# Position distances from one minus the gate, rounded by ScalarE; turned outputs in a bank of their own; position logits of two units at once in the ring

## The chip, the cores and the metric
One core of a Trainium2 chip runs the whole decoder layer as one program. The metric is the device time of one execution in microseconds (us); the number given for a kernel is the median of its runs.

## The reference
x is 1x2048x256. The part that the change touches is the self-attention with 16 heads of 64, whose logits get a contextual position term (the cross-attention to 1601 context rows, the low-rank GELU network and the three layer norms are not touched):

```python
G = sigmoid(sim)                                   # sim = q k^T / 8, per head 2048 x 2048
P = flip(cumsum(flip(G)))                          # sum of the gates from j to the end of the row
P = minimum(P, 63)
E = einsum('bnc,ct->bnt', q, pos_emb)              # 64 position logits for each query
w = P - floor(P)
sim = sim + w * E[ceil(P)] + (1 - w) * E[floor(P)]
out = softmax(sim) @ v
```

Behind some 176 keys from the end the sum of gates is over 63 in all rows, so that the term is the constant E[63] there. The kernel subtracts E[63] from the table and works on the last W = 176 keys only. It keeps the lowest sum in satmin, and `general_attention` does the whole attention again if some row is not saturated at the window's start; with these inputs it doesn't.

## The kernel before, in words
A **unit** is 128 queries of one head, a **pair** is two units u = 0, 1. There are G = 16 x 8 = 128 pairs, and each engine runs its own program over them (`body(g)`; on SP, ScalarE (`act`), TensorE (`pe`) and VectorE (`dve`)). All order is written out by hand with semaphores; `wait_apart` is a wait as an instruction of its own. PSUM holds four banks of logits (`Sc`, one unit at a time), one of position logits (`near`), two of a ring (`ring`) and one of outputs (`out`). Ring slots are numbered: what TensorE puts there counts up `slot_full`, ScalarE's copy out of it counts up `slot_out`, and slot k waits until slot k - 2 is out.

In the pass for pair g, TensorE (L592 on) does: the logits of unit 0 in two halves (L544, each when ScalarE has read those banks for the unit before); the turn of pair g-1's unit 0 (L575: the outputs lie there as 64x2 halves by keys of even and odd tiles, and a matmul with `fold` adds and turns them); the 16 transposes of unit 1 of pair g-1 in four slots s0 to s3 (L552); its outputs (L566), interrupted by the queries and keys of the next head (`project`, L500) and the values (`project_values`, L513); the logits of unit 1; the turn of unit 1 of pair g-1; the transposes of unit 0 of pair g; the **window** (L522, position logits of pair g+2: 128 queries x 240 columns, 176 keys and 64 table entries, twice, both from the partitions 64 to 127 and into one bank); the outputs of unit 0.

ScalarE copies the ring out (`transposed` L409, `project` L368, `values` L382), scales the turned outputs by the inverse sum (`scale`, L418), copies `out` to `halves` (L424), does tanh on the window (L388), copies the table to z (L392), and the exponentials (L430, two halves of a row, each with its sum).

VectorE takes the maxima (L748), adds the correction to the last 175 logits (L755), finds the bias (L765), and works out the corrections of the next pair over 128x352 (two units of 176 keys): it scans tanh to 2P - 1 (L674), rounds (L680), runs a second scan that holds the floors to steps of one (L689), takes distances from a ramp (L695), makes seven bit masks (L702), shifts the table by each bit (`copy_predicated`, L712), takes clamp, fractions and slopes (L717, L722, L728), and shifts slopes and values by the last bit (L735, once per unit). GpSimd multiplies fractions and slopes (L348); VectorE adds (L742). SP loads the queries: `load_far` for the window two pairs ahead, `load_now` for the logits.

The loop has three stages: pairs 0 to 111 with project and values, 112 to 119 without values, 120 to 127 without both (`late`).

Of the kernel before, what the change touches and what calls it, by code (L numbers as in the profile page):

```python
# [44 lines left out]
RND2 = 1.5 * 2.0 ** 24  # L45
# [3 lines left out]
SATURATED = 2.0 * T - 3.0  # L49
SLOTS0 = 8 + 2 * PAIRS - 6  # L50
SLOTS = 12
LATE_SLOTS = 10
# [66 lines left out]
def attention(nc, A):  # L119
# [3 lines left out]
    with ExitStack() as ctx:  # L123
# [22 lines left out]
        q_far = sb("q_far", [P, 2 * P])  # L146
# [5 lines left out]
        twoP = sb("twoP", [P, 2, W])  # L152
        cut = sb("cut", [P, 2, W])
        rnd = sb("rnd", [P, 2, W])
        flo = rnd
        frac = cut
        dist = sb("dist", [P, 2, W], I16)
        mask = sb("mask", [P, BITS, 2, W], I16)
# [3 lines left out]
        ones = sb("ones", [P, W])  # L162
        twos = sb("twos", [P, W])
        ramp = sb("ramp", [P, 2, W])

        posx = cut[:, 0, 0:T]
        rampi = prod[:, :, :].bitcast(I32)
# [4 lines left out]
        near = pb("near", [P, BANK])  # L172
        ring = [pb(f"ring{i}", [P, BANK]) for i in range(2)]
        out = pb("out", [P, BANK])
        xs = probs[:, :, :].rearrange("p a (t d) -> p (a t) d", d=D)


        near_win = near[:, 0:2 * (W + T)].rearrange("p (i w) -> p i w", w=W + T)[:, :, 0:W]
        near_E = near[:, 0:2 * (W + T)].rearrange("p (i w) -> p i w", w=W + T)[:, :, W:W + T]
# [20 lines left out]
        halves_out = sem("halves_out")  # L200
        summed = sem("summed")
# [4 lines left out]
        shifted = sem("shifted")  # L206
        prod_done = sem("prod_done")
# [5 lines left out]
        def queries(h, odd, block):  # L213

            half = slice(0, C) if odd else slice(C, P)
            return qk[half, h % 2, int(odd), bass.ds(block // 2 * STEP, STEP)]

        SCANS = ["scan 0", "scan 1", "round"]
        SC = len(SCANS)
        CHAIN = (["floor 0", "floor 1", "distances", "cut"]  # L220
                 + [f"mask {b}" for b in reversed(range(BITS))]
                 + [f"shift {b}" for b in reversed(range(1, BITS))]
                 + ["fractions", "slopes", "last shift"])
# [3 lines left out]
        def _(sp):  # L227
# [51 lines left out]
            def body(g, odd, late=False, first=False, tile=True, far=True, head=False):  # L279
                base = slots_before(g, late)  # L280
                if head:

                    wait_apart(sp, out_full, g * 2, waited)
                    load_values(g)
# [1453 lines left out]
```

## Time and profile before
| | us |
|---|---|
| median of 3 runs | 2650.29 (2649.49 to 2651.93) |
| the profiled execution, its own time | 2652.94 |
| its span, first to last instruction | 2651.1 |
| TensorE busy | 2472.1 (93%) |
| VectorE busy | 2006.4 (76%) |
| ScalarE busy | 1615.9 (61%) |
| GpSimd busy | 190.4 (7%) |

The busy times are of the whole span; attention takes the first 2177 us of it, where all of the change lies. TensorE's granted clock has a mean of 0.985 of full speed. PE is TensorE's matmuls, PEld its weight loads, DVE VectorE, ACT ScalarE, POOL GpSimd.

### The profile page before, as it was taken

The page shows a single profiled execution, that of the slowest core. Times are in us where ns is not written, and L with a number is a line of the kernel's source. Part 1 is how long each engine was busy: PE and PEld are TensorE (multiplying, and loading weights), DVE is VectorE, ACT ScalarE, POOL GpSimd, SP SyncE. Part 2 cuts the span into 40 slices and gives each one's busy share as a digit, 9 for nine tenths or more (in the row PEclk, how much of TensorE's full clock was granted, in tenths as well). Part 3 has the DMA queues.
Part 4 walks back from the last instruction along what each step waited for, and adds up shares of the span by engine and source line. Part 5 has one row for each costly group of instructions (what it writes and reads, how often), then busy time and mean ns, then how long its engine had stood idle before and what let it go on. Part 6 is the DMA issues. An engine that isn't in the chain of part 4 may idle for free. (4 is left out here: it accounts for less than half of the span.)

```text
span 2651.1 us, 64197 instructions
## 1 busy us (share of the span) xinstructions
PE 2472.1 (93%) x18687; PEld 1691.1 (64%) x18687; DVE 2006.4 (76%) x5179; ACT 1615.9 (61%) x3383; POOL 190.4 (7%) x289
## 2 busy tenths in 40 slices
PE   7999998999899989998999999999999988999997
PEld 5666665666566656666666566666666656777776
DVE  6888888888888888888888888888899960232322
ACT  4666666666666666666666666666666663444442
POOL 0000000000000000000000000000000000111111
PEclk9999999999999999999999999999999998999998
DMA  2010101010101010100101110101001002100100
GB/s 68 20 33 20 34 20 32 20 34 20 32 20 34 20 32 21 32 21 21 29 24 29 25 29 24 29 24 29 22 21 40 21 17 68 34 26 34 36 26 6
DMA packets 96567, 74.74 MB, mean 28 GB/s; under 512 B 24590, under 2 KB 92303, under 8 KB 96464
## 3 DMA queue, kind: packets, MB, share of 16 engines
q1 hardware_dynamic: 96464, 73.15, 10.1%
q8 instruction: 90, 1.47, 0.2%
q14 instruction: 13, 0.11, 0.0%
HBM read 14.26 MB, written 2.10 MB: 6 GB/s over the span
## 5 line engine op out<-in xcount | busy, mean ns | idle before, releaser
L748 DVE TENSOR_REDUCE mx<-Sc 128x1 f32<-128x1024 f32 x512 | 621.5, 1214 | 160.2 <-PE Sc L544 159.7
L552 PE MATMUL ring<-ident,probs 128*128 128x128 f32 x4096 | 620.9, 284 | 115.2 <-ACT attn L418 65.3
L409 ACT ACTIVATE probsT<-ring 128x512 f32<-128x512 f32 x1024 | 584.7, 596 | 132.1 <-PE ring L552 129.2
L552 PEld LDWEIGHTS ring<-ident,probs 128*128 128x128 f32 x4096 | 446.3, 145 | 258.3 <-ACT attn L418 127.0
L430 ACT ACTIVATE probs<-Sc,nbias 128x1024 f32<-128x1024 f32 x512 | 565.6, 1117 | 4.7 <-DVE nbias L765 4.7
L544 PE MATMUL Sc<-qk,q_now 64*128 64x512 f32 x2048 | 539.4, 637 | 22.4 <-issue 16.0
L566 PE MATMUL out<-probsT,V_now 128*64 128x128 f32 x8192 | 530.0, 277 | 0.0
L566 PEld LDWEIGHTS out<-probsT,V_now 128*64 128x64 f32 x8192 | 439.5, 137 | 76.3 <-ACT probsT L409 57.9
L712 DVE COPY_PREDICATED z<-mask,z 128x224 f32<-128x224 int16 (+5 forms) x768 | 389.7, 507 | 34.4
L418 ACT ACTIVATE attn<-ring,rsum 128x64 f32 (+1 forms) x256 | 80.3, 314 | 436.5 <-PE ring L575 420.7
L544 PEld LDWEIGHTS Sc<-qk,q_now 64*128 64x128 f32 x2048 | 173.6, 188 | 217.8 <-issue 217.8
L348 POOL TENSOR_TENSOR prod<-cut,z 128x350 f32<-128x350 f32 x128 | 118.3, 924 | 2036.2 <-DVE z L735 2036.2
L575 PEld LDWEIGHTS ring<-fold,halves 128*128 128x128 f32 x512 | 76.9, 189 | 197.0 <-issue 114.6
L702 DVE TENSOR_SCALAR mask<-dist 128x352 int16<-128x352 int16 x896 | 155.3, 245 | 6.6
L500 PE MATMUL ring<-xT,wqk 128*128 (+1 forms) x512 | 144.3, 404 | 2.1 <-DMA wv<-in_L_attn_Wkv_dram 1.3
L522 PE MATMUL near<-qk,q_far 64*128 64x240 f32 x512 | 137.5, 389 | 2.0 <-DMA q_far<-qk 2.0
L674 DVE TENSOR_TENSOR_SCAN twoP<-tanh,ones 128x176 f32<-128x176 f32 x256 | 119.6, 510 | 12.6 <-ACT tanh L388 12.6
L735 DVE COPY_PREDICATED z<-mask,z 128x348 f32<-128x348 int16 x256 | 125.4, 544 | 0.1
L689 DVE TENSOR_TENSOR_SCAN rnd<-twos,rnd 128x176 f32<-128x176 f32 x256 | 118.9, 506 | 0.1
L424 ACT ACTIVATE halves<-out 128x128 f32<-128x128 f32 x256 | 72.1, 282 | 70.3 <-PE out L566 70.3
L575 PE MATMUL ring<-fold,halves 128*128 128x64 f32 x512 | 112.3, 301 | 1.6 <-ACT probs L430 1.2
L430 ACT ACTIVATION_READ_ACCUMULATOR probs<-Sc,nbias 128x1 f32 x512 | 108.1, 211 | 0.0
(116 smaller groups left out, 2301.8 us busy)
## 6 DMA issues: line engine op xcount, KB each, us to landing
q_now<-qk SPq DMA_DIRECT2D x256, 64.0 KB, 2.0
xv<-xT SPq DMA_DIRECT2D x113, 128.0 KB, 2.2
q_far<-qk SPq DMA_DIRECT2D x128, 64.0 KB, 1.9
V_now<-V SPq DMA_DIRECT2D x16, 512.0 KB, 3.2
at<-attn SPq DMA_DIRECT2D x16, 512.0 KB, 3.2
probs<-in_x_dram SPq DMA_DIRECT2D x4, 512.0 KB, 5.3
wqk<-in_L_attn_Wq_dram SPq DMA_DIRECT2D x32, 64.0 KB, 2.1
xin<-in_x_dram SPq DMA_DIRECT2D x16, 128.0 KB, 2.8
```

Of the source, the lines that this page charges most:

```text
L409: nc.scalar.activation(probsT[:, u, 4 * s:4 * s + 4, :], ring[k % 2][:, :].rearrange("p (t q) -> p t q", q=P), ACT.Copy).then_inc(slot_out, 1)
L430: nc.scalar.activation(probs[:, u, cols], Sc[:, cols], ACT.Exp, bias=nbias[:, u:u + 1], accum_out=sums[:, u, half:half + 1]).then_inc(exp_ ...
L500: last = nc.tensor.matmul(ring[k % 2][:, 0:STEP], wqk[:, c, at:at + 2 * C], xT[:, c, bass.ds(b * STEP, STEP)], start=c == 0, stop=c == DC - 1)
L522: last = nc.tensor.matmul(near[:, i * (W + T):(i + 1) * (W + T)], q_far[C:P, i * P:(i + 1) * P], qk[C:P, par, 1, HALF - W:QK], start=True, ...
L544: last = nc.tensor.matmul(Sc[:, bank * BANK:(bank + 1) * BANK], q_now[rows, u * P:(u + 1) * P], qk[rows, par, r, cols], start=True, stop=True)
L552: last = nc.tensor.transpose(ring[k % 2][:, j * P:(j + 1) * P], probs[:, u, (4 * s + j) * P:(4 * s + j + 1) * P], ident[:, :])
L566: last = nc.tensor.matmul(out[half:half + C, 0:P], V_now[:, token_tile(t), :], probsT[:, u, t, :], start=t < 2, stop=t >= NT - 2)
L575: nc.tensor.matmul(ring[k % 2][:, 0:C], halves[:, u, :], fold[:, :], start=True, stop=True).then_inc(slot_full, 1)
L702: nc.vector.tensor_scalar(mask[:, b, :, :], dist[:, :, :], 2 << b, None, ALU.bitwise_and).then_inc(shifted, 1)
L712: nc.vector.copy_predicated(z[:, 0, :, 0:k], mask[:, b, :, 0:k], z[:, 0, :, 1 << b:W]).then_inc(shifted, 1)
L735: last = nc.vector.copy_predicated(z[:, :, i, 1:W - 1], mask[:, 0, i, 1:W - 1].unsqueeze(1).broadcast_to([P, 2, W - 2]), z[:, :, i, 2:W])
L748: nc.vector.tensor_reduce(mx[:, u, half:half + 1], Sc[:, half * HALF:(half + 1) * HALF], AX.X, ALU.max).then_inc(dve_unit, 1)
```

## The change
The scan adds up what each gate leaves (1 + tanh of minus half the logit is twice 1 - G), so that it gives the distance to shift by, not the position: 2 x (count - P) - 1. ScalarE makes these sums (`steps`), rounds them by adding 1.5 x 2^23 (`positions`) and writes them as whole numbers (`distances`). VectorE's rounding, second scan, ramp, clamp and distances are gone. A distance that isn't clamped can reach past the table, so all 176 columns of z are now filled for each pair: ScalarE copies the table to `near_table_in`, GpSimd copies that to z (`start_table`). Fractions are taken against the distance without its last bit, so the last bit is shifted in the slopes alone, in one instruction. The turned outputs get the bank that `near` had (`turns`, with semaphores `turned` and `scaled`), and each turn stands between the transposes s1 and s2. The window's two units now read the partitions 64 to 127 and 0 to 63 (`q_far` by unit, `k_near` a copy of the keys) and write the two ring banks, between the outputs and the second unit's logits; transposes wait until ScalarE has read both parts. SP loads each window's queries in two parts, `load_near` once per head, and the head's values behind them.

```diff
+TO_STEPS = 0.5 - 2.0 ** -23
+SATURATED = -(2.0 * (W - T + 1) - 1.0)
+SLOTS = 10
...
-def __init__(self, first=False, proj=True):
-    self.turn0 = 0
-    self.last = [1, 2, 3, 4]
-    at = 6 if first else 5
-    self.qk, self.values = at, at + 1
-    at += 2 if proj else 0
-    self.turn1 = at
-    at += 0 if first else 1
+def __init__(self, proj=True):
+    self.last = [0, 1, 2, 3]
+    self.qk, self.values = 4, 5
+    at = 6 if proj else 4
     self.now = [at, at + 1, at + 2, at + 3]
...
+    near_win = rings[:, :, 0:W]
+    near_E = rings[:, :, W:W + T]
...
-        sp.dma_start(q_far[C:P, :], queries(h, odd, t)).then_inc(far_in, 16)
+        for i in range(2):
+            rows = slice(0, C) if i else slice(C, P)
+            sp.dma_start(q_far[rows, :], queries(h, odd, t, i)).then_inc(far_in, 16)
+    def load_near(h):
+        sp.dma_start(k_near[:, h % 2, 0:W], qk[C:P, h % 2, 1, HALF - W:HALF]).then_inc(k_near_in, 16)
...
+    def start_table(c):
+        pool.wait_ge(near_out, c * 2 + 2)
+        if not (isinstance(c, int) and c == 0):
+            wait_apart(pool, corr_done, c, waited)
+        nc.gpsimd.tensor_copy(z[:, 0, :, :], near_table_in[:, :, :]).then_inc(z_in, 1)
...
-                             near_win, ACT.Tanh, scale=0.5).then_inc(near_out, 1)
-    def near_table(c):
-        nc.scalar.activation(z[:, 0, :, W - T:W], near_E, ACT.Copy).then_inc(near_out, 1)
+                             near_win, ACT.Tanh, scale=-0.5).then_inc(near_out, 1)
+    def steps(c):
+        act.wait_ge(near_out, c * 2 + 1)
+        nc.scalar.activation(passed[:, :, :], tanh[:, :, :], ACT.Identity,
+                             bias=bias_one[:, :]).then_inc(step_in, 1)
+    def positions(c):
+        act.wait_ge(scanned, c * SC + SC)
+        nc.scalar.activation(rnd[:, :, :], behind[:, :, :], ACT.Identity, scale=TO_STEPS,
+                             bias=bias_rnd[:, :]).then_inc(rounded, 1)
+    def distances(c):
+        act.wait_ge(rounded, c + 1)
+        nc.scalar.activation(dist[:, :, :], rnd[:, :, :], ACT.Identity, scale=2.0,
+                             bias=bias_dist[:, :]).then_inc(dist_in, 1)
+    def near_table(c, first=False):
+        if not first:
+            wait_apart(act, z_in, c, waited)
+        nc.scalar.activation(near_table_in[:, :, W - T:W], near_E, ACT.Copy).then_inc(near_out, 1)
...
-    def scale(g, u, base, k):
+    def scale(g, u):
         h, t = g // PAIRS, g % PAIRS
         act.wait_ge(rsum_done, g * 2 + u + 1)
-        wait_apart(act, slot_full, base + k + 1, waited)
-        nc.scalar.activation(attn[:, t * 2 + u, bass.ds(h * C, C)], ring[k % 2][:, 0:C], ACT.Copy,
-                             scale=rsum[:, u:u + 1]).then_inc(slot_out, 1)
+        wait_apart(act, turned, g * 2 + u + 1, waited)
+        nc.scalar.activation(attn[:, t * 2 + u, bass.ds(h * C, C)], turns[:, 0:C], ACT.Copy,
+                             scale=rsum[:, u:u + 1]).then_inc(scaled, 1)
...
-        at = Slots(first, proj)
+        at = Slots(proj)
+        if near:
+            positions(g + 1)
         if not first:
             empty_halves(g - 1, 0)
-            scale(g - 1, 0, base, at.turn0)
+        if near:
+            distances(g + 1)
+        if not first:
             transposed(1, base, at.last)
-        if near:
-            act.wait_ge(corr_done, g + 1)
-            near_table(g + 1)
+            scale(g - 1, 0)
         exps(g, 0)
-        if not first:
-            empty_halves(g - 1, 1)
         if proj:
             project(g + PAIRS, not odd, base, at.qk, alone=not val)
         if val:
             values(g, base, at.values)
         if not first:
-            scale(g - 1, 1, base, at.turn1)
+            empty_halves(g - 1, 1)
+        if far:
+            near_tanh(g + 2)
+            near_table(g + 2)
+            steps(g + 2)
         transposed(0, base, at.now)
-        if far:
-            act.wait_ge(scanned, g * SC + (SC + 2))
-            near_tanh(g + 2)
+        if not first:
+            scale(g - 1, 1)
...
-        pe.wait_ge(far_in, c * 16 + 16)
+        pe.wait_ge(far_in, c * 32 + 32)
         for i in range(2):
-            last = nc.tensor.matmul(near[:, i * (W + T):(i + 1) * (W + T)], q_far[C:P, i * P:(i + 1) * P],
-                                    qk[C:P, par, 1, HALF - W:QK], start=True, stop=True)
+            rows = slice(0, C) if i else slice(C, P)
+            keys = k_near[:, par, :] if i else qk[C:P, par, 1, HALF - W:QK]
+            last = nc.tensor.matmul(rings[:, i, 0:W + T], q_far[rows, :], keys,
+                                    start=True, stop=True)
         last.then_inc(near_full, 1)
...
-    def turn(g, u, base, k):
+    def turn(g, u, evicted=True):
         pe.wait_ge(halves_out, g * 2 + u + 1)
-        pe.wait_ge(slot_out, base + k - 1)
-        nc.tensor.matmul(ring[k % 2][:, 0:C], halves[:, u, :], fold[:, :],
-                         start=True, stop=True).then_inc(slot_full, 1)
-    def body(g, odd, par, late=False, first=False, proj=True, val=True, far=True, far_par=None):
+        if evicted:
+            wait_apart(pe, scaled, g * 2 + u, waited)
+        nc.tensor.matmul(turns[:, 0:C], halves[:, u, :], fold[:, :],
+                         start=True, stop=True).then_inc(turned, 1)
+    def transposes_and_turn(g, u, base, slots, turned_unit, first=False, evicted=True):
+        for s in range(4):
+            transposes(u, base, slots, s)
+            if s == 1 and not first:
+                turn(g, turned_unit, evicted)
...
-            turn(g - 1, 0, base, at.turn0)
-            for s in range(4):
-                transposes(1, base, at.last, s)
+            transposes_and_turn(g - 1, 1, base, at.last, 0, evicted=not second)
             outputs(g - 1, 1, base, at.last, tiles=range(FIRST))
         if proj:
             weights_at = (g // PAIRS) * 64 + 128 if val else H * 64 - 16
...
             project_values(g + PAIRS, base, at.values)
         if not first:
             outputs(g - 1, 1, base, at.last, tiles=range(FIRST, NT))
+        if far:
+            wait_apart(pe, slot_out, base + at.now[0], waited)
+            window(g + 2, par if far_par is None else far_par)
         wait_apart(pe, exp_done, g * 4 + 1, waited)
         logits(par, 1, 0)
         wait_apart(pe, exp_done, g * 4 + 2, waited)
         logits(par, 1, 1)
-        if not first:
-            turn(g - 1, 1, base, at.turn1)
-        for s in range(4):
-            transposes(0, base, at.now, s)
         if far:
-            pe.wait_ge(near_out, g * 2 + 4)
-            window(g + 2, par if far_par is None else far_par)
+            wait_apart(pe, near_out, g * 2 + 6, waited)
+        transposes_and_turn(g - 1, 0, base, at.now, 1, first)
         outputs(g, 0, base, at.now, empty=not first)
...
-        dve.wait_ge(near_out, c * 2 + 1)
+        dve.wait_ge(step_in, c + 1)
         for i in range(2):
-            nc.vector.tensor_tensor_scan(twoP[:, i, ::-1], tanh[:, i, ::-1], ones[:, :], -1.0,
+            nc.vector.tensor_tensor_scan(behind[:, i, ::-1], passed[:, i, ::-1], zeros[:, :], -1.0,
                                          ALU.add, ALU.add).then_inc(scanned, 1)
-    def round_positions(c):
+    def saturation(c):
         after_scan(c, "scan 1")
-        nc.vector.tensor_scalar(rnd[:, :, :], twoP[:, :, :], 2.0 * T - 3.0, RND2,
-                                ALU.min, ALU.add).then_inc(scanned, 1)
-        nc.vector.tensor_tensor(satmin[:, :], satmin[:, :], twoP[:, :, 0], ALU.min)\
-            .then_inc(ramped, 1)
-    def scan_floors(c):
-        after_scan(c, "round")
-        for i in range(2):
-            nc.vector.tensor_tensor_scan(flo[:, i, ::-1], twos[:, :], rnd[:, i, ::-1], RND2 - 2.0,
-                                         ALU.add, ALU.min).then_inc(shifted, 1)
-    def distances(c):
-        after(c, "floor 1")
-        nc.vector.tensor_tensor(dist[:, :, :], ramp[:, :, :], flo[:, :, :],
-                                ALU.subtract).then_inc(shifted, 1)
+        nc.vector.scalar_tensor_tensor(satmin[:, :], behind[:, :, 0], -1.0, satmin[:, :],
+                                       ALU.mult, ALU.min).then_inc(ramped, 1)
     def masks(c):
-        after(c, "distances")
+        dve.wait_ge(dist_in, c + 1)
+        nc.vector.tensor_scalar(even[:, :, :], dist[:, :, :], (4 << BITS) - 4, 1,
+                                ALU.bitwise_and, ALU.bitwise_or).then_inc(shifted, 1)
         for b in reversed(range(BITS)):
             nc.vector.tensor_scalar(mask[:, b, :, :], dist[:, :, :], 2 << b, None,
                                     ALU.bitwise_and).then_inc(shifted, 1)
+    def fractions(c):
+        after(c, "even")
+        nc.vector.tensor_tensor(frac[:, :, :], behind[:, :, :], even[:, :, :],
+                                ALU.subtract).then_inc(shifted, 1)
     def shift(c, b):
         top = b == BITS - 1
-        after(c, f"mask {b}" if top else f"shift {b + 1}")
+        after(c, "fractions" if top else f"shift {b + 1}")
         if top:
-            wait_apart(dve, near_out, c * 2 + 2, waited)
+            wait_apart(dve, z_in, c + 1, waited)
         k = W - (1 << b)
         nc.vector.copy_predicated(z[:, 0, :, 0:k], mask[:, b, :, 0:k],
                                   z[:, 0, :, 1 << b:W]).then_inc(shifted, 1)
...
     def last_shift(c):
         after(c, "slopes")
-        for i in range(2):
-            last = nc.vector.copy_predicated(
-                z[:, :, i, 1:W - 1], mask[:, 0, i, 1:W - 1].unsqueeze(1).broadcast_to([P, 2, W - 2]),
-                z[:, :, i, 2:W])
-        last.then_inc(shifted, 1)
+        nc.vector.copy_predicated(z[:, 1, :, 1:W - 1], mask[:, 0, :, 1:W - 1],
+                                  z[:, 1, :, 2:W]).then_inc(shifted, 1)
...
-        if chain:
-            scan_floors(c)
         window_max(g, 0)
         bias(g, 0)
-        if chain:
-            distances(c)
         if not first:
             add_halves(g - 1, 1)
         if chain:
-            clamp(c)
+            masks(c)
         if not first:
-            invert(g - 1, 1, base)
+            invert(g - 1, 1, used=not second)
         if chain:
-            masks(c)
-            shift(c, 6)
-            shift(c, 5)
+            fractions(c)
+            for b in reversed(range(2, BITS)):
+                shift(c, b)
         half_max(g, 1, 0)
-        if chain:
-            shift(c, 4)
         add_window(g, 1)
-        if chain:
-            shift(c, 3)
         window_max(g, 1)
-        if chain:
-            shift(c, 2)
         bias(g, 1)
+        if scan:
+            scan_positions(c + 1)
         if chain:
             shift(c, 1)
-            fractions(c)
+        if scan:
+            saturation(c + 1)
+        if chain:
             slopes(c)
         add_halves(g, 0)
-        if scan:
-            scan_positions(c + 1)
-        invert(g, 0, None if first else base + (Slots().turn0 + 1))
-        if scan:
-            round_positions(c + 1)
         if chain:
             last_shift(c)
-    dve.wait_ge(ramped, 2)
+        invert(g, 0, used=not first)
```

## Rows read from the trace of the kernel before
**Rows 1.** The page's first part: busy us (share of the span), instructions of each engine.
```profile
PE 2472.1 (93%) x18687; PEld 1691.1 (64%) x18687; DVE 2006.4 (76%) x5179; ACT 1615.9 (61%) x3383; POOL 190.4 (7%) x289
```
**Rows 2.** By stretch: length, busy PE, PEld, DVE, ACT, POOL, granted clock, DMA.
```profile
1000.21:1016.82 16.61, 15.67 (x129) 10.50 (x129) 14.76 (x39) 11.16 (x25) 0.92 (x1) 1.00 0.08 21
1971.66:1987.64 15.98, 15.25 (x126) 9.89 (x124) 14.71 (x39) 10.98 (x23) 0.89 (x2) 1.00 0.05 12
2098.93:2114.29 15.36, 14.36 (x120) 9.20 (x120) 14.62 (x39) 10.41 (x23) 0.92 (x1) 1.00 0.06 13
```
**Rows 3.** Timeline, TensorE: start us, length, engine, line, operation, count [idle before].
```profile
1000.21 1.14 PE L552 MATMUL ring<-ident,probs 128*128 128x128 f32 x8 [0.35 <-ACT attn L418]
1001.55 0.66 PE L552 MATMUL ring<-ident,probs 128*128 128x128 f32 x4 [0.20 <-ACT probsT L409]
...
1005.70 1.99 PE L544 MATMUL Sc<-qk,q_now 64*128 64x512 f32 x8
1007.61 0.43 PE L575 MATMUL ring<-fold,halves 128*128 128x64 f32 x2
...
1010.62 0.70 PEld L522 LDWEIGHTS near<-qk,q_far 64*128 64x128 f32 x4 [0.17 <-issue]
1011.62 1.97 PE L566 MATMUL out<-probsT,V_now 128*64 128x128 f32 x32
1013.52 2.14 PE L544 MATMUL Sc<-qk,q_now 64*128 64x512 f32 x8
1014.50 0.33 PEld L544 LDWEIGHTS Sc<-qk,q_now 64*128 64x128 f32 x4 [0.68 <-issue]
1015.59 0.43 PE L575 MATMUL ring<-fold,halves 128*128 128x64 f32 x2
1015.86 0.61 PE L552 MATMUL ring<-ident,probs 128*128 128x128 f32 x4
```
**Rows 4.** Timeline of the same pass, ScalarE.
```profile
1002.25 0.60 ACT L409 ACTIVATE probsT<-ring 128x512 f32<-128x512 f32 x1 [0.26 <-PE ring L552]
1002.74 0.27 ACT L392 ACTIVATE z<-near 128x128 f32<-128x128 f32 x1
...
1006.29 0.47 ACT L368 ACTIVATE qk<-ring,qk_scale 128x256 f32 x1 [0.20 <-issue]
1006.74 0.28 ACT L382 ACTIVATE V<-ring 128x128 f32 x1
...
1011.73 0.47 ACT L388 ACTIVATE tanh<-near 128x352 f32<-128x352 f32 x1 [0.41 <-PE near L522]
1012.09 1.11 ACT L430 ACTIVATE probs<-Sc,nbias 128x1024 f32<-128x1024 f32 x1
...
1014.17 0.21 ACT L430 ACTIVATION_READ_ACCUMULATOR probs<-Sc,nbias 128x1 f32 x1
1014.26 0.28 ACT L424 ACTIVATE halves<-out 128x128 f32<-128x128 f32 x1
1016.45 0.31 ACT L418 ACTIVATE attn<-ring,rsum 128x64 f32 x1 [1.90 <-PE ring L575]
1016.66 0.59 ACT L409 ACTIVATE probsT<-ring 128x512 f32<-128x512 f32 x1
```
**Rows 5.** Timeline of the same pass, VectorE.
```profile
1006.87 1.22 DVE L748 TENSOR_REDUCE mx<-Sc 128x1 f32<-128x1024 f32 x1 [1.13 <-PE Sc L544]
```
**Rows 6.** Groups of instructions: busy us, mean ns of one | idle before.
```profile
L689 DVE TENSOR_TENSOR_SCAN rnd<-twos,rnd 128x176 f32<-128x176 f32 x256 | 118.9, 506 | 0.1
L348 POOL TENSOR_TENSOR prod<-cut,z 128x350 f32<-128x350 f32 x128 | 118.3, 924 | 2036.2 <-DVE z L735 2036.2
L695 DVE TENSOR_TENSOR dist<-ramp,rnd 128x352 int16<-128x352 f32 x128 | 67.2, 525 | 8.9 <-DVE rnd L689 0.2
L1365 ACT ACT_TABLE_LOAD x29 | 37.2, 1283 | 0.5
L1423 ACT ACTIVATE QT<-ring,bq 128x128 f32<-128x128 f32 x32 | 10.0, 363 | 14.9 <-PE ring L1605 14.9
```

More of the change, by code:

```diff
@@ L44 @@
 VW = C + 1
[L45 removed]
+RND = 1.5 * 2.0 ** 23
+TO_STEPS = 0.5 - 2.0 ** -23
 TAIL = N - W
@@ L211, in attention, with queries @@
         UNIT = 3
-        def queries(h, odd, block):
+        def queries(h, odd, block, unit=None):
             half = slice(0, C) if odd else slice(C, P)
-            return qk[half, h % 2, int(odd), bass.ds(block // 2 * STEP, STEP)]
-        SCANS = ["scan 0", "scan 1", "round"]
+            if unit is None:
+                return qk[half, h % 2, int(odd), bass.ds(block // 2 * STEP, STEP)]
+            return qk[half, h % 2, int(odd), bass.ds(block // 2 * STEP + unit * P, P)]
+        SCANS = ["scan 0", "scan 1"]
         SC = len(SCANS)
-        CHAIN = (["floor 0", "floor 1", "distances", "cut"]
-                 + [f"mask {b}" for b in reversed(range(BITS))]
+        CHAIN = (["even"] + [f"mask {b}" for b in reversed(range(BITS))] + ["fractions"]
                  + [f"shift {b}" for b in reversed(range(1, BITS))]
-                 + ["fractions", "slopes", "last shift"])
+                 + ["slopes", "last shift"])
         CH = len(CHAIN)
@@ L277, in _, with body @@
             load_values(0)
-            def body(g, odd, late=False, first=False, tile=True, far=True, head=False):
+            def body(g, odd, late=False, first=False, tile=True, far=True, head=False, near=False):
                 base = slots_before(g, late)
-                if head:
-                    wait_apart(sp, out_full, g * 2, waited)
-                    load_values(g)
                 if far:
@@ L398, in _ @@
                     near_tanh(0)
-                    near_table(0)
+                    near_table(0, first=True)
+                    steps(0)
+                    positions(0)
+                    distances(0)
                 if s == WINDOW1:
-                    act.wait_ge(scanned, 2)
                     near_tanh(1)
+                    near_table(1)
+                    steps(1)
             def transposed(u, base, slots):
@@ L779, in add_halves, with body @@
                                         ALU.add).then_inc(summed, 1)
-            def body(g, late=False, first=False, chain=True, scan=True):
+            def body(g, late=False, first=False, second=False, chain=True, scan=True):
                 c = g + 1
@@ L841, in _ @@
             scan_positions(1)
-            round_positions(1)
+            saturation(1)
             body(0, first=True)
-            with dve.Fori(1, LASTP) as g:
+            body(1, second=True)
+            with dve.Fori(2, LASTP) as g:
                 body(g)
```

130 lines of the change are left out of this document (72 added, 58 removed).

## The prediction
> **What bounds the kernel now.** I read the views in this order. The page's first part: TensorE is busy for 93% of the span, VectorE for 76%, ScalarE for 61% [rows 1]. The busy time by stretch: one pass of the attention loop (one pair of query units) lasts 16.61 us for the first 112 pairs, and in it TensorE is busy for 15.67, VectorE for 14.76, ScalarE for 11.16; it lasts 15.98 us for the eight pairs without values and 15.36 us for the last ones [rows 2]. So TensorE and VectorE are both nearly full there, and a gain must shorten both. After the loops, from about 2177 us, nothing is touched.
>
> The timeline then gives the order inside one pass. TensorE's idle places are all around the turn (L575): transposes s0 follow it, s1 waits for the ring slot that the turn holds and that ScalarE empties late: turn at 1015.59, scale only at 1016.45 [rows 3, 4]. From turn to s3 is 2.57 us in the one half (1015.59 to 1018.16, one pass after 1001.55). VectorE pauses at the first maximum of the second unit, for 1.13 us [rows 5]: its slack per pass.
>
> **The change on TensorE.** Pieces of a pass, from issue to next issue [rows 3]: logits of a unit 1.91 (1005.70 to 1007.61); a turn 0.27 (1015.59 to 1015.86); four transposes 0.57 (two fours from 1000.21 to 1001.55, less the 0.20 of waiting); s3 itself with outputs, project and values, up to the second unit's logits, 4.15 (1001.55 to 1005.70); outputs of the other unit 1.90 (1011.62 to 1013.52); the window 1.00 (1010.62 to 1011.62).
>
> The window's two matmuls now stand in different row halves and banks. No row has a window done so; the nearest are the logits, which pair rows in that way: 1.91 for two pairs of 512 columns, so 0.95 for a pair, of which 240/512 is 0.45 if all scales and 0.95 if nothing does. I take 0.53, nearest to the scaled end because the logits are the same form. Unpaired it stays 1.00.
>
> The turn moves between s1 and s2, into its own bank. It fills the time in which s2 would wait for s0's copy: a copy starts 0.70 after its transposes' issue and lasts 0.60 [rows 4], and TensorE follows in some 0.05, so s2 may start at 1.35 against 1.14 + 0.27 = 1.41. From s0 to s3 is then 1.98, both halves. TensorE's own work is 1.98 + 4.15 + 0.53 + 1.91 to the second s0, and 1.98 + 0.57 + 1.90 + 1.91 back: 14.9 us.
>
> **Which waits take over.** I follow the path through ScalarE, whose order the change rewrites. From the issue of s3: copy at +0.70 (1001.55 to 1002.25), next instruction 0.49 later (1002.74), so +1.19 [rows 3, 4]; the scale now stands here, 0.21 (1016.45 to 1016.66), exponentials at +1.40.
>
> First half: both exponentials take 2.17 (1012.09 to 1014.26), then project 0.45 and values 0.28 [rows 4], all three ahead of the window, because the window takes both ring banks. With 0.12 of signalling (the exponentials' last sum ends at 1014.38, TensorE moves at 1014.50) the window starts at +4.42. TensorE alone would be there at +4.15. Then window 0.53, logits 1.91, and s0.
> Second half: exponentials at +1.40, and second-half logits 2.41 after them (1012.09 to 1014.50) at +3.81, against 0.57 + 1.90 + 0.95 = +3.42 for TensorE alone; from there to the turn was 1.09 (1014.50 to 1015.59) and is now to s0.
> The closed path is 2 x 1.98 + 4.42 + 0.53 + 1.91 + 3.81 + 1.09 = 15.72 us, longer than TensorE's 14.9. This is the new bound: ScalarE between the transposes and the exponentials, not the row of matmuls.
>
> What can be added to it I bound from rows. (a) Project has a 0.20 pause before it in the loop, after the short copy of halves [rows 4]; behind the exponentials, which are long, it may be hidden. 0 to 0.20: I take 0.20, what the row shows. (b) The scale starts 0.43 after its matmul's modelled end (1015.59 + 0.43 to 1016.45), a copy 0.04 after its own, so up to 0.39 of preparation may appear, twice; or none, if it is done during the copy ahead of it. I take 0.05 each, near nothing, as the 0.49 of the copy ahead covers it. (c) TensorE gets four separate new waits (the turns' bank twice, both ring banks free, positions read); the idle before a change of weights is 0.17 [rows 3], so 0 to 0.68. I take 0: three of them are met long before. Sum 0.30, pass 16.02; ends 15.72 and 17.38.
>
> **The other work of the change, and what hides it.** ScalarE gets three more passes over 128x352: steps, positions, distances. The nearest row is the tanh of that shape, 0.47; issue to issue I use project's 0.45 [rows 4], which also has a per-partition operand. Positions and distances with halves between them need about 1.1 to 1.3 us in the gap from the end of the exponentials (1.40 + 2.17 = +3.57) to the first copy of the next transposes (3.81 + 1.09 + 0.70 = +5.60): 2.0 us, so 0.7 is left. Tanh, table and steps run beside the 1.91 of logits that follow the window: tanh starts 1.11 after the window's issue now (1010.62 to 1011.73) and about 0.6 then, table read by +1.3, where s0 needs the banks at 0.53 + 1.91 = +2.44. Cost nothing; if the cover goes, each costs up to 0.45.
> By the Trainium skill (ScalarE: Activation LUTs, What ACT_TABLE_LOAD costs) a [128,1] bias operand adds about 93 ns to an ACTIVATE, so 0.56 for each of the three as an estimate; the rows with and without such an operand (L368 0.47 for 256 columns, tanh 0.47 for 352) fit, and the sum stays as it is, since 0.3 more is inside the gap.
> In the trace the window's banks were its own; now 0.27 of the 0.47 saved (+4.42 against +4.15) goes to waiting for the ring. The Trainium skill (TensorEngine Tiling, PSUM Bottleneck) says that tiling speeds up TensorE "but not PSUM evacuation": read strictly, the whole 0.47 would go, and the pass would be 16.2.
>
> VectorE loses the two floor scans (118.9 us over 128 pairs, 0.93 each), the distances 0.52 [rows 6], and rounding, clamp and one of two last shifts, passes of no more than the distances' width, at 0 to 0.52; it gets one 16-bit operation, again at most 0.52. Between 0.9 and 3.0 less; I take 2.3, since all of these are real passes. Idle would then be 1.13 + 2.3 - 0.59 = 2.8 us of a pass. Its five upper shifts now stand in a row, each waiting for the one before; some 0.1 of waiting each eats 0.5 of the 2.8. So VectorE's saving is worth nothing by itself: it lets TensorE run ahead. If it were late after all, each bias would be late by what is missing; I see 1 us of room ahead of either.
> GpSimd gets a copy of 128x352 per pair; the product of that shape with two inputs takes 0.92 [rows 6], so 0 to 0.92, between the corrections and shift 6, where VectorE has two maxima's halves, sums and masks to do, over 3 us: nothing. SP issues one more query load per pair, and the far queries now have a whole pass before their window: nothing. One load per head for the near keys, waited for on SP alone, behind the next query loads: nothing.
>
> **The sum.** 110 full pairs: (16.61 - 16.02) x 110 = 65 us. Eight pairs without values: their path is shorter by 0.28, 15.74 against 15.98: 2 us. In late pairs, without project, the window no longer waits for ScalarE: 1.98 x 2 + (0.57 + 1.90 + 0.53 + 1.91) + (3.81 + 1.09) = 13.8, and with the scales and a nearly full VectorE I take 14.1, against 15.36; six of them, 7 us. The start, where VectorE's first chain stands alone, loses two pairs' floors (3.7 with roundings) and gains the hops to ScalarE: I take 2 us. Together 76. The profiled execution took 2652.94 us (span 2651.1), so 2577; the median of the runs lies 2.65 below it: **2574 us**.
>
> **Rivals.**
> A, TensorE alone is the bound: if ScalarE's waits vanish, 14.9 per pass, 1.7 x 110 + 20 = 207 less than the median: 2443. For it, that ScalarE is idle for a third of a pass; against, the path above has no slack. 7%.
> B, the window isn't paired (a shared bank access or the queue keeps them serial): 0.47 back in each of 118 passes, 55 us: 2629. Against it the logits. 7%.
> C, preparation shows on all three places of (a) and (b), 0.98: pass 16.70, 10 us lost, 11 won elsewhere: 2650, no change. 7%.
> D, slower: the two handovers through ScalarE. The scale with its 0.39 ahead of either pair of exponentials, project's 0.20 ahead of the window, and half of TensorE's 0.68: 1.32, pass 17.04, 0.43 x 110 = 47 more, less 11: 2686. It decides from additions of 1.0 per pass on. For it, that exponentials were started straight behind a copy and now have a two-wait instruction ahead; against, copies of 0.49 that cover it. 16%.
> E, Identity needs a table of its own: two loads of 1.28 us [rows 6] in each pass, there and back, of which the gap hides 0.7: 1.86 x 128 = 238, so 2812. Against: the biased copy L1423 runs between exponentials, and no load stands at its line [rows 6]. 2%.
>
> **How the numbers follow.** The forecast case has 61%, its own range 2539 (additions of 0: 0.89 x 110 = 98, and 13) to 2620 (additions of 0.7). Over all, A and most of D are left out: 2535 to 2665. A difference of 0.2%, 5 us, is what a measurement of this kernel can tell. Faster: forecast, A, B: 75%; same: most of C, 7%; slower: D, E and a part of C: 18%.
>
> **What would show it.** A pass of 16.0 us in the timeline; the window of about 0.5 with a wait for V's copy (L382) of 0.3 to 0.5 ahead of it; no wait for attn's scale in the transposes; a wait of TensorE for probs (L430) ahead of the second-half logits; VectorE idle for 2 to 3 us a pass. It is wrong if a pass shows ScalarE full between exponentials and copies, VectorE late with a bias, or POOL's copy ahead of shift 6.

## The result, and the profile after
The changed kernel takes **2493.8 us** in the median (2491.3 to 2495.5, 4 runs) against 2649.9 for the kernel before on the same chip (4 runs): ratio 0.941, 95% interval 0.9394 to 0.9426. The forecast of 2574 had the direction and the new bound right, but only half of the gain: 76 us instead of 156. The measured time is outside the range of 2535 to 2665.

The page's first part of the changed kernel answers to [rows 1]; under it, as in [rows 2], stand one full pass and one late pass: length, busy PE, PEld, DVE, ACT, POOL, granted clock, DMA.

```profile
PE 2340.9 (94%) x18687; PEld 1674.2 (67%) x18687; DVE 1814.7 (73%) x4542; ACT 1745.9 (70%) x3767; POOL 253.6 (10%) x417
```
```profile
999.40:1014.80 15.40, 14.75 (x128) 10.40 (x129) 13.27 (x34) 12.19 (x28) 1.41 (x2) 1.00 0.09 22
...
1937.00:1951.60 14.60, 13.08 (x124) 9.04 (x122) 13.12 (x34) 11.52 (x27) 1.41 (x2) 1.00 0.06 14
```
A full pass has gone from 16.61 to 15.40 us, VectorE in it from 14.76 to 13.27, ScalarE from 11.16 up to 12.19. TensorE's busy time fell by 0.92: the window is busy for some 0.7 instead of 1.07, and turns (0.43 to 0.33) and transposes (2.4 to 2.24 for the sixteen) are shorter, twice each.

Where the 159.6 us between the two spans lie, by the starts of unit 0's logits in each pass (L544 before, L607 now): the first logits come 3.9 us later (34.5 against 30.7), the first pass is 3.3 shorter; passes 1 to 110 give 146; the eight without values go from 16.08 to 15.19 on average, 7 us; six late ones from 15.31 to 14.55, 5 us; the rest is 2.

The timeline of one pass, TensorE, answers to [rows 3] (8 transposes are two ring slots):

```profile
1001.56 1.09 PE L615 MATMUL rings<-ident,probs 128*128 128x128 f32 x8
1002.90 0.91 PEld L615 LDWEIGHTS rings<-ident,probs 128*128 128x128 f32 x8 [0.22 <-ACT probsT L463]
...
1007.91 0.46 PE L581 MATMUL rings<-qk,q_far 64*128 64x240 f32 x1 [0.31 <-ACT V L412]
1007.92 0.47 PE L581 MATMUL rings<-k_near,q_far 64*128 64x240 f32 x1
...
1008.21 0.40 PEld L607 LDWEIGHTS Sc<-qk,q_now 64*128 64x128 f32 x4
1008.41 1.89 PE L607 MATMUL Sc<-qk,q_now 64*128 64x512 f32 x8
1010.23 1.09 PE L615 MATMUL rings<-ident,probs 128*128 128x128 f32 x8
1011.58 1.15 PE L615 MATMUL rings<-ident,probs 128*128 128x128 f32 x8
1012.65 1.97 PE L629 MATMUL out<-probsT,V_now 128*64 128x128 f32 x32
1014.80 2.23 PE L607 MATMUL Sc<-qk,q_now 64*128 64x512 f32 x8 [0.18 <-ACT probs L484]
1015.87 0.33 PEld L607 LDWEIGHTS Sc<-qk,q_now 64*128 64x128 f32 x4 [0.77 <-issue]
1016.96 1.10 PE L615 MATMUL rings<-ident,probs 128*128 128x128 f32 x8
```
The stall behind the turn is gone; what is left is 0.22, in which s2 waits for s0's copy. The window's two matmuls start 0.01 apart and run side by side, and TensorE now waits where the forecast said: 0.31 for the values' copy (L412) ahead of the window, 0.18 for the exponentials (L484) ahead of the logits. ScalarE in the same pass answers to [rows 4]:

```profile
1004.58 0.31 ACT L472 ACTIVATE attn<-turns,rsum 128x64 f32 x1
1004.78 1.12 ACT L484 ACTIVATE probs<-Sc,nbias 128x1024 f32<-128x1024 f32 x1
...
1006.96 0.49 ACT L398 ACTIVATE qk<-rings,qk_scale 128x256 f32 x1
1007.31 0.30 ACT L412 ACTIVATE V<-rings 128x128 f32 x1
...
1013.25 0.31 ACT L472 ACTIVATE attn<-turns,rsum 128x64 f32 x1
1013.45 1.12 ACT L484 ACTIVATE probs<-Sc,nbias 128x1024 f32<-128x1024 f32 x1
```
No gap stands ahead of the scale (L472) nor ahead of project (L398).

### The profile page after: what moved, and what is told of

Same layout as the page of the kernel before. It is cut to its first block and busy times, and to the rows that moved or that the text cites. A ratio compares the mean times of both kernels' runs of the same rounds, so it can differ in the third digit from the quotient of the medians.

```text
span 2491.5 us, 64093 instructions
## 1 busy us (share of the span) xinstructions
PE 2340.9 (94%) x18687; PEld 1674.2 (67%) x18687; DVE 1814.7 (73%) x4542; ACT 1745.9 (70%) x3767; POOL 253.6 (10%) x417
## 5 line engine op out<-in xcount | busy, mean ns | idle before, releaser
L463 ACT ACTIVATE probsT<-rings 128x512 f32<-128x512 f32 x1024 | 556.4, 595 | 334.9 <-PE rings L615 334.9
L615 PEld LDWEIGHTS rings<-ident,probs 128*128 128x128 f32 x4096 | 434.3, 141 | 269.0 <-issue 194.2
L615 PE MATMUL rings<-ident,probs 128*128 128x128 f32 x4096 | 572.9, 283 | 22.1 <-ACT probs L484 1.2
L607 PE MATMUL Sc<-qk,q_now 64*128 64x512 f32 x2048 | 529.6, 615 | 46.8 <-ACT probs L484 26.5
L484 ACT ACTIVATE probs<-Sc,nbias 128x1024 f32<-128x1024 f32 x512 | 566.9, 1121 | 8.6 <-DVE nbias L813 8.6
L607 PEld LDWEIGHTS Sc<-qk,q_now 64*128 64x128 f32 x2048 | 188.1, 187 | 232.5 <-issue 231.5
L557 PE MATMUL rings<-xT,wqk 128*128 (+1 forms) x512 | 144.3, 404 | 5.1 <-DMA wv<-in_L_attn_Wkv_dram 1.7
L742 DVE TENSOR_TENSOR_SCAN behind<-passed,zeros 128x176 f32<-128x176 f32 x256 | 120.7, 513 | 11.3 <-ACT passed L424 11.3
L581 PE MATMUL rings<-qk,q_far 64*128 64x240 f32 x256 | 85.2, 413 | 40.9 <-ACT V L412 35.3
L484 ACT ACTIVATION_READ_ACCUMULATOR probs<-Sc,nbias 128x1 f32 x512 | 109.6, 214 | 0.0
L557 PEld LDWEIGHTS rings<-xT,wqk 128*128 128x128 f32 x512 | 86.7, 189 | 34.0 <-issue 22.7
L1540 PE MATMUL Sc<-K2T,QT 128*128 128x512 f32 (+1 forms) x256 | 98.2, 518 | 1.2 <-ACT QT L1459 1.2
L803 DVE TENSOR_TENSOR Sc<-Sc,prod 128x175 f32<-128x175 f32 x256 | 87.9, 343 | 14.1
L1605 PE MATMUL acc<-Vx,prT 128*128 128x257 f32 (+1 forms) x416 | 96.0, 380 | 0.0
```

Of the source, the lines that this page charges most:

```text
L463: nc.scalar.activation(probsT[:, u, 4 * s:4 * s + 4, :], ring[k % 2][:, :].rearrange("p (t q) -> p t q", q=P), ACT.Copy).then_inc(slot_out, 1)
L484: nc.scalar.activation(probs[:, u, cols], Sc[:, cols], ACT.Exp, bias=nbias[:, u:u + 1], accum_out=sums[:, u, half:half + 1]).then_inc(exp_ ...
L557: last = nc.tensor.matmul(ring[k % 2][:, 0:STEP], wqk[:, c, at:at + 2 * C], xT[:, c, bass.ds(b * STEP, STEP)], start=c == 0, stop=c == DC - 1)
L607: last = nc.tensor.matmul(Sc[:, bank * BANK:(bank + 1) * BANK], q_now[rows, u * P:(u + 1) * P], qk[rows, par, r, cols], start=True, stop=True)
L615: last = nc.tensor.transpose(ring[k % 2][:, j * P:(j + 1) * P], probs[:, u, (4 * s + j) * P:(4 * s + j + 1) * P], ident[:, :])
L742: nc.vector.tensor_tensor_scan(behind[:, i, ::-1], passed[:, i, ::-1], zeros[:, :], -1.0, ALU.add, ALU.add).then_inc(scanned, 1)
```

## The experiments
All times below are medians of 4 to 10 runs, with the kernel before run beside them on each chip (medians 2647.9 to 2648.7). "Pass" is the median time from one unit 0 logits to the next. The expectations name their theories by letters: P says that the closed path through TensorE and ScalarE sets the pass, T that TensorE's own work does, V that VectorE's does. A range in brackets is the 95% interval of the ratio.

**e1, late scales.** ScalarE's two scales leave their place between copies and exponentials.

```diff
                 transposed(1, base, at.last)
-                scale(g - 1, 0)
             exps(g, 0)
...
                 empty_halves(g - 1, 1)
+                scale(g - 1, 0)
...
             transposed(0, base, at.now)
+            exps(g, 1)
             if not first:
                 scale(g - 1, 1)
-            exps(g, 1)
```


> The changed kernel with the scale of unit 0 behind values and halves, and that of unit 1 behind its exponentials, so that exponentials follow the transposes' copies directly. Theory P (the pass of 15.40 us is the closed path transposes, copies, scale, exponentials, project and values, window, logits): each scale takes 0.20 out of the path (4.58 to 4.78 in the changed kernel's timeline), twice: pass 15.0, 127 passes, about 50 us less than the changed kernel: 2444. Rival T (TensorE's own work with its handovers is the bound): nothing, 2494. Rival V (VectorE's handovers are the bound, its relief gave the gain): nothing, 2494.

Measured: 2450.4 us, ratio to the kernel before 0.9254 (0.923 to 0.9278); pass 14.97. Theory P stands: its pass of 15.0 is met to 0.03 us, its time of 2444 to 6 us. T and V are out. ScalarE and TensorE in this run:

```profile
1005.74 1.08 ACT L463 ACTIVATE probsT<-rings 128x512 f32<-128x512 f32 x2 [0.26 <-PE rings L615]
1006.72 1.11 ACT L484 ACTIVATE probs<-Sc,nbias 128x1024 f32<-128x1024 f32 x1
1008.03 0.33 PEld L607 LDWEIGHTS Sc<-qk,q_now 64*128 64x128 f32 x4 [0.19 <-issue]
1008.06 2.22 PE L607 MATMUL Sc<-qk,q_now 64*128 64x512 f32 x8
```
The exponentials follow the copies, and the logits no longer wait for them by name. This version beats the change: 43 us less.

**e2, window not paired.** Both units' queries in the partitions 64 to 127.

```diff
-            rows = slice(0, C) if i else slice(C, P)
-            keys = k_near[:, par, :] if i else qk[C:P, par, 1, HALF - W:QK]
-            last = nc.tensor.matmul(rings[:, i, 0:W + T], q_far[rows, :], keys,
+            keys = qk[C:P, par, 1, HALF - W:QK]
+            last = nc.tensor.matmul(rings[:, i, 0:W + T], q_far[C:P, i * P:(i + 1) * P], keys,
```


> The changed kernel with both units' position logits read from the partitions 64 to 127, so that the two matmuls can't run side by side; everything else stays. Theory P and rival T: the window takes about 1.0 instead of 0.50, pass 15.9, 126 windows: 60 us more, 2554. Rival V: the window is hidden behind VectorE, under 15 us more.

Measured: 2548.2 us, ratio 0.9625 (0.9604 to 0.9646), pass 15.78, so 0.39 for the pairing; V is out. P and T expected the same, and both 0.1 too much. The rows show what they left out: a first matmul of the logits now starts beside the window.

```profile
1001.77 0.46 PE L579 MATMUL rings<-qk,q_far 64*128 64x240 f32 x1 [0.30 <-ACT V L411]
1001.99 0.66 PE L605 MATMUL Sc<-qk,q_now 64*128 64x512 f32 x1
1002.07 0.77 PE L579 MATMUL rings<-qk,q_far 64*128 64x240 f32 x3
```
From the window to s0 it is 2.71 (to 1004.48), against 2.32 in the change. The wait for the values' copy ahead of the window is the same, 0.30.

**e3, turn first.**

```diff
+            if not first:
+                turn(g, turned_unit, evicted)
             for s in range(4):
                 transposes(u, base, slots, s)
-                if s == 1 and not first:
-                    turn(g, turned_unit, evicted)
```


> The changed kernel with each turn ahead of the transposes s0 instead of between s1 and s2, still in its own bank. Theory P: s2 waits for s0's copy anyway (0.22 behind the turn now), so the turn fills time that is idle; ahead of s0 it costs its 0.27 in full, twice: pass 15.94, 68 us more, 2562. Rival T: the same 0.27 less the filled idle that comes back, also about 0.5. Rival V: under 15 us more.

Measured: 2549.6 us, ratio 0.9639 (0.9615 to 0.9663), pass 15.83: 0.22 for each turn, where P expected 0.27 (and 2562 us).

```profile
1002.21 0.43 PE L639 MATMUL turns<-fold,halves 128*128 128x64 f32 x2
1002.48 1.04 PE L615 MATMUL rings<-ident,probs 128*128 128x128 f32 x8
1003.77 1.14 PE L615 MATMUL rings<-ident,probs 128*128 128x128 f32 x8 [0.25 <-ACT probsT L463]
```
The turn costs its 0.27 ahead of s0, and 0.05 comes back: s2 follows s0 by 1.29 instead of 1.34. The place of the turn is worth about as much as the pairing.

**e4, the new order with the old arithmetic.** The kernel keeps banks, window, turns and the table copy; VectorE gets back second scan, ramp, rounding, clamp and both last shifts, in the old order, and ScalarE loses its three passes.

```diff
-                if near:
-                    positions(g + 1)
...
-                if near:
-                    distances(g + 1)
...
-                    steps(g + 2)
...
             add_window(g, 0)
+            if chain:
+                scan_floors(c)
             window_max(g, 0)
             bias(g, 0)
+            if chain:
+                distances(c)
...
+                clamp(c)
```


> The changed kernel's order of TensorE, its banks, paired window and GpSimd's table copy, but the arithmetic of the kernel before on VectorE in its old order (second scan, ramp, rounding, clamp, two last shifts) and without the three ScalarE passes. Theory P: VectorE now needs 15.48 us of each pass (16.61 less its pause of 1.13), just over the path's 15.40: pass 15.5 to 15.7, 2505 to 2530; most of the gain is the banks and the order. Rival V: VectorE back at its old length holds the pass near 16.3 to 16.6, 2610 to 2650; the gain is the relief of VectorE.

Measured: 2677.8 us, ratio 1.0111 (1.009 to 1.0132), pass 16.9. Both theories missed (P expected 2505 to 2530, V 2610 to 2650): it is slower than the kernel before, though VectorE is idle for 2.1 us of the pass. Its timeline:

```profile
1000.24 1.22 DVE L793 TENSOR_REDUCE mx<-Sc 128x1 f32<-128x1024 f32 x1 [1.83 <-PE Sc L584]
1007.96 1.21 DVE L793 TENSOR_REDUCE mx<-Sc 128x1 f32<-128x1024 f32 x1
1010.01 1.06 DVE L734 TENSOR_TENSOR_SCAN rnd<-twos,rnd 128x176 f32<-128x176 f32 x2
1010.99 1.19 DVE L793 TENSOR_REDUCE mx<-Sc 128x1 f32<-128x1024 f32 x1
1012.21 0.16 DVE L810 TENSOR_REDUCE nbias<-mx 128x1 f32<-128x2 f32 x1
1012.40 1.11 ACT L466 ACTIVATE probs<-Sc,nbias 128x1024 f32<-128x1024 f32 x1 [1.36 <-DVE nbias L810]
1015.53 0.46 PE L558 MATMUL rings<-qk,q_far 64*128 64x240 f32 x1 [1.76 <-ACT V L414]
1017.11 1.23 DVE L793 TENSOR_REDUCE mx<-Sc 128x1 f32<-128x1024 f32 x1 [1.44 <-PE Sc L584]
```
From unit 1's first maximum to unit 0's VectorE works without a pause (1000.24 to 1007.96, 7.72). Then unit 0's bias comes 4.41 later, with the second scan ahead of it; exponentials, project and values, the window and its wait, the logits: 4.74 more until VectorE may take unit 1's maximum. 7.72 + 4.41 + 4.74 = 16.87. So VectorE's pause of 1.44 is the late bias that has come round: the window stands behind the exponentials, the logits behind the window. In the old order the same bias, with the same scan ahead of it, had 0.55 to spare before ScalarE was free for the exponentials, and the window didn't stand behind them. Two lines of the kernel before:

```profile
1002.19 0.16 DVE L765 TENSOR_REDUCE nbias<-mx 128x1 f32<-128x2 f32 x1
...
1002.90 1.12 ACT L430 ACTIVATE probs<-Sc,nbias 128x1024 f32<-128x1024 f32 x1
```

**e7, the same work, the second scan behind the bias.**

```diff
             add_window(g, 0)
-            if chain:
-                scan_floors(c)
             window_max(g, 0)
             bias(g, 0)
             if chain:
+                scan_floors(c)
                 distances(c)
```


> The new order with the old arithmetic (2678 us, pass 16.87), with the second scan behind unit 0's bias instead of ahead of it; VectorE does exactly the same work. Theory Q (with the new order the bound of that kernel is a closed path maxima, bias of unit 0, exponentials, project and values, window, logits, maxima of unit 1, rest of VectorE's pass): 0.95 comes off the path, pass 15.9, about 105 us less, 2573. Rival W (VectorE's total of work is the bound): no change, 2678.

Measured: 2580.2 us, ratio 0.9745 (0.9726 to 0.9764), pass 16.06 in the median and 16.1 on average: 97.5 us less with not one instruction less.

```profile
1008.78 1.21 DVE L793 TENSOR_REDUCE mx<-Sc 128x1 f32<-128x1024 f32 x1
...
1012.21 0.15 DVE L810 TENSOR_REDUCE nbias<-mx 128x1 f32<-128x2 f32 x1
1012.44 0.94 DVE L734 TENSOR_TENSOR_SCAN rnd<-twos,rnd 128x176 f32<-128x176 f32 x2
```
From unit 0's first maximum to its bias it is 3.58 instead of 4.41, so 0.83 comes off, and the pass is 0.81 to 0.83 shorter. Q stands, with 0.95 expected; W is out. And this kernel, new order with old arithmetic, is 68 us faster than the kernel before.

**e5, the old order with less work for VectorE.** The kernel before, leaving out the second scan, the clamp, and one of the two last shifts, so that its position term isn't exact.

```diff
-        CHAIN = (["floor 0", "floor 1", "distances", "cut"]
+        CHAIN = (["distances"]
...
-            if chain:
-                scan_floors(c)
...
-            if chain:
-                clamp(c)
```


> The kernel before, leaving out the second scan, the clamp and the value half of the last shift (so its position term is not exact), about 1.8 us less work for VectorE in each pass; order, banks and window as before. Theory P' (the old order is bound by TensorE with its stalls around the turn, not by VectorE): pass stays 16.6, 2640 to 2650; only the start is some 3 us shorter. Rival V (VectorE's relief is worth something by itself): pass 15.0 to 15.5, 2450 to 2520.

Measured: 2643.7 us, ratio 0.9987 (0.9975 to 0.9999), pass 16.61 as before. VectorE's busy time over two passes, then who waits:

```profile
1000.00:1033.20 33.20, 31.33 (x258) 20.99 (x257) 26.66 (x70) 22.32 (x50) 1.85 (x2) 1.00 0.08 20
```
```profile
DVE mx L733 <- PE Sc L544: 297.1, 254, 4.9
```
13.33 a pass instead of 14.76, and VectorE's wait for the logits is 297.1 us in all, where it was 159.7 before: what it saved it waits. Alone, the relief is worth 4 us (0 to 7 by the interval). P' stands, V is out.

**e8, ScalarE's passes out of their cover.**

```diff
-            if near:
-                positions(g + 1)
             if not first:
                 empty_halves(g - 1, 0)
-            if near:
-                distances(g + 1)
             if not first:
                 transposed(1, base, at.last)
+            if near:
+                positions(g + 1)
+                distances(g + 1)
+            if not first:
                 scale(g - 1, 0)
```


> The changed kernel with ScalarE's positions and distances behind the transposes' copies and ahead of unit 0's exponentials, instead of in the gap before the copies; the same instructions. Theory P: they leave their cover and stand on the path: 0.48 and 0.62, so pass 16.4 to 16.5, 2620 to 2635. Rival T (TensorE's own work bounds): under 0.3 per pass more, below 2535.

Measured: 2638.2 us, ratio 0.9969 (0.9951 to 0.9986), pass 16.49, as P expected; the time is 3 us over P's range.

```profile
1009.29 0.58 ACT L430 ACTIVATE rnd<-behind,bias_rnd 128x352 f32<-128x352 f32 x1
1009.90 0.59 ACT L436 ACTIVATE dist<-rnd,bias_dist 128x352 int16<-128x352 f32 x1
1010.40 0.29 ACT L472 ACTIVATE attn<-turns,rsum 128x64 f32 x1
```
1.11 on the path (1009.29 to 1010.40), 1.10 per pass: all of the change's gain but some 10 us hangs on where two of ScalarE's passes stand.

**e6, e1 with VectorE's shifts spread.**

```diff
-                for b in reversed(range(2, BITS)):
-                    shift(c, b)
+                shift(c, 6)
+                shift(c, 5)
+                shift(c, 4)
             half_max(g, 1, 0)
+            if chain:
+                shift(c, 3)
             add_window(g, 1)
             window_max(g, 1)
+            if chain:
+                shift(c, 2)
             bias(g, 1)
```


> The kernel with late scales (2450 us, pass 14.97) with VectorE's shifts 3 and 2 put behind the first and the second maximum of unit 1, instead of all five in front. Theory P: in full passes VectorE has 0.5 to 0.8 us of room, so nothing there; in the seven late passes of 14.55, where ScalarE waits 1.06 for unit 1's bias, some 0.5 less each: 3 to 4 us less in all, 2446, hardly told from 2450. Rival V: each full pass gets shorter too, 2400 to 2440.

Measured: 2445.8 us, ratio 0.9248 (0.9228 to 0.9268), which the intervals don't tell from e1. Pass 14.99, unchanged; the late passes go from 14.56 to 13.92. V is out once more.

**e9, the change again.** No edit.

> The changed kernel again, unchanged, for the five places where an outer loop of TensorE turns (once in 16 pairs). In the first profile of the change those five passes last 18.3 to 18.7 us and four of the five passes after them are not longer than the rest; in the kernel before they last 19.6 to 20.2 and each next pass is 1.6 to 3.1 longer, with a stretch at half clock near each. Theory H (half clock after a turn is chance, not the change's doing): the second profile of the same kernel shows it at another number of places than one, and its span differs by 2 to 3 us per place. Rival: the change ends it for good: again at most one place.

Measured: 2495.3 us, ratio 0.9426 (0.9402 to 0.9449). Four of the five turns of the outer loop have a stretch at half clock now, and four next passes are 1.4 to 2.4 us longer, where the first profile had one of each. So the number of such places differs between two runs of one program, as H says. H's price was too high: passes 1 to 110 are together 5 us longer, 1.7 for each further place instead of 2 to 3, and the spans differ by 1.0 only, because start, first pass and tail are shorter by 4. Stretches of 7 us at such a turn, first of the first profile, then of this one (the eighth figure is the granted clock as a share of full):

```profile
1405.00:1412.00 7.00, 6.28 (x42) 4.44 (x42) 5.01 (x16) 3.49 (x8) 0.48 (x1) 1.00 0.03 7
```
```profile
1403.00:1410.00 7.00, 3.92 (x13) 1.37 (x10) 2.26 (x5) 2.37 (x7) 0.94 (x1) 0.66 0.17 42
```

## Why the prediction was wrong
**The bound was right.** The path named in the forecast closes on the measured pass. From the rows above (s3 is the second of its eight, 0.57 after their start): s0 to s3 1.91, to the window 4.44, window 0.50, logits 1.82, s0 to s3 1.92, to the second-half logits 3.72, to s0 1.09: 15.40. e1 takes from it just what the scales are on it, 2 x 0.21; e8 puts 1.11 on it and gets 1.10. VectorE's idle time in a pass, 2.13, is near the forecast of 2.3 too.

**The step that failed is the sum of the pass**, 16.02 instead of 15.40, in two terms of nearly one size: 0.30 of additions that aren't there, and 0.32 of the path itself. Without any additions the forecast was 2539, still 45 us above the measured time; so the range had no room for an error in the path.
- "What can be added to it": I took 0.30, a pause of 0.20 ahead of project and 0.05 of preparation for each scale. Nothing of it is there. Project starts 1.09 after the second exponential, as the exponentials allow, and e1 gets back 0.21 per scale, its bare issue. The pause of 0.20 in [rows 4] stood behind a copy of 0.28, and project now stands behind the exponentials. I take it that what made the pause is now done during the long instruction ahead, but no run shows that; distances follow the same short copy without a pause (1000.71, then 1000.87).
- The path itself, 15.72 instead of 15.40, by these pieces. From s3 to the exponentials it is 1.31, not 1.40, twice (0.18 less). From s0 to s3 it is 1.91 and 1.92, not 1.98 (0.13 less): s2 starts 1.34 after s0, when s0's copy is done, which the forecast had at 1.35 and passed over for a sum of transposes and turn, 1.41. The turn lies within that wait and costs nothing. The logits behind the window take 1.82, not 1.91 (0.09 less); their first weights are loaded during the window (1008.21). The window takes 0.50, not 0.53 (0.03 less). Against that, the rest of the stretch to the window is 0.11 longer: the values' handover took 0.30, not 0.12, project and values together 0.65, not 0.73, and the exponentials 2.18, not 2.17. In all 0.32. Each piece was taken from an edge in the old order with another neighbour.

0.62 x 110 = 68 us. The rest of the 80 that were missed: 11 us at the five turns of the outer loop, of which 5 come back in e9, the same program, so that about half is chance and the rest open; 5 for the eight pairs without values (15.19, forecast 15.74); less 2 to 3 each at the start and in the late passes, where VectorE's shifts in a row hold unit 1's bias back. ScalarE in a late pass of the change:

```profile
1936.90 0.31 ACT L472 ACTIVATE attn<-turns,rsum 128x64 f32 x1
1938.27 1.11 ACT L484 ACTIVATE probs<-Sc,nbias 128x1024 f32<-128x1024 f32 x1 [1.06 <-DVE nbias L813]
```
The exponentials wait 1.06 for the bias; spreading the shifts (e6) gave 0.64 a pass.

**The window** is paired, as taken (rival B out; e2: 0.39 per pass of its 0.47). The Trainium skill (TensorEngine Tiling, PSUM Bottleneck) says that tiling doesn't speed up PSUM evacuation; read strictly, the pairing would have brought nothing. The rows do show TensorE waiting 0.31 for the ring's copy ahead of the window, but e2 waits 0.30 there unpaired, and 0.39 of the pairing remain. So that wait comes with the window's place in the ring, not with the pairing.

**VectorE.** "Worth nothing by itself: it lets TensorE run ahead" is right in both halves, but I did not price the second. e5: in the old order it is worth 4 us. In the new order it is worth much more, but how much hangs on one instruction's place: with the second scan ahead of unit 0's bias, order and banks alone are 30 us slower than before (e4); with it behind the bias they are 68 us faster (e7), and the new arithmetic adds 86 to that. So the parts can't be added up, and e4 by itself doesn't show that the new order needs the relief. A check of the pass for VectorE's own closed path, with the window in it, would have shown that the old arithmetic in its old sequence doesn't fit; I had only looked at its slack.

**Rivals.** A (TensorE alone, 14.9 a pass) is out: 15.40, and e1 moves it by ScalarE's scales alone. C and D rest on the same additions as the 0.30 and fell with it. E is out: the profile has no table load among the loop's lines. The far query loads, GpSimd's copy and its products show no wait in the pass, as said: the copy lasts 0.48 and ends at 1002.86, 3.5 us before shift 6.

## What to carry to other kernels
When several engines hand work round in a loop, sum each closed path issue to issue and take each edge from a row in which the same two neighbours stand in the same order; a pause seen behind one neighbour may be gone behind another. Here the relief of VectorE was worth 4 us in the old order and 86 to 184 in the new one. The new order without it lost 30 us or won 68, by the place of one scan. So test the corners, and more than one placing in each. Then look at what stands between a copy and the next producer on the path: moving two scales off that place gave 43 us more, moving two passes into it took 144.

## What the runs showed of the hardware that was not expected
Once in 16 pairs TensorE's program turns its outer loop and pauses for 2.9 to 3.5 us; two such places in the first profile of the change:

```profile
402.78 1.04 PE L629 MATMUL out<-probsT,V_now 128*64 128x128 f32 x16
407.31 1.23 PE L607 MATMUL Sc<-qk,q_now 64*128 64x512 f32 x2 [3.49 <-issue]
...
658.30 1.99 PE L607 MATMUL Sc<-qk,q_now 64*128 64x512 f32 x8 [3.43 <-issue]
```
At some of these turns the granted clock is at its half level, 1.2 GHz, when the logits of unit 0 start, and they take 3.25 to 3.79 us; at others (658.30) it stays at 2.4 GHz and they take 1.99. The kernel before had the half level at five of five, the change at one and at four of five in two profiles of the same program, e6 at two. The length of the pause doesn't decide it: 3.43 went without, 2.94 (e9) with it. What does is open. Between the two profiles of the change it makes 5 us of the loop's time.

ScalarE's three biased passes over 128x352 last 0.59 to 0.61, the tanh of that shape 0.46, so 0.13 or more between them. The Trainium skill (ScalarE: Activation LUTs, What ACT_TABLE_LOAD costs) gives some 0.09 for a per-partition operand. The tanh reads PSUM and the passes read SBUF, so these rows don't tell the bias's share from that of the place read. Issue to issue the passes take 0.48 to 0.62.
